# A four-stage graph network on one core: the loop of every engine in each edge pass moved to a multiple of 256 instruction slots

## The reference

```python
x = _layernorm(x + layer(x, edge_index, ...))
# layer 0: two spline convolutions   msg = (1-u)*h0[src] + u*h1[src]; mean over dst
# layer 1: attention; sum, mean and max of messages over dst and again over src
# layer 2: three GCN convolutions, widths 16, 16, 32   sum over dst of norm * h[row]
# layer 3: softmax attention over dst  out = sum(alpha * (z[src] + e)) + x
```

## The kernel before

| from, to | A-B | B-C | C-D | D-E | E-F | F-G | G-H |
|---|---|---|---|---|---|---|---|
| POOL | 185 | 368 | (C-E) 475 | | 165 | 165 | 341 |
| ACT | 103 | 82 | 34 | 129 | 63 | 74 | 118 |
| DVE | 174 | 364 | 259 | 274 | 159 | 181 | 248 |
| PE | 686 | 491 | 281 | 593 | 410 | 548 | 974 |
| SP | 34 | 85 | 40 | 33 | 23 | 23 | 51 |

## Time and profile before

### The profile page before, as it was taken

The page is one execution under the profiler, slowest core; times in us unless marked ns, Lnnn a source line. Parts: engine busy times, 40 slices in busy tenths (PEclk is TensorE's granted clock), DMA queues, the critical chain, the costliest instruction groups (busy, mean ns, idle before and its releaser), DMA issues. The chain is left out here.

```text
span 20591.8 us, 194797 instructions
## 1 busy us (share of the span) xinstructions
PE 7375.4 (36%) x49884; PEld 6283.1 (31%) x49884; DVE 8998.8 (44%) x25746; ACT 2698.1 (13%) x7499; POOL 12080.9 (59%) x11797
## 2 busy tenths in 40 slices
PE   3444444444322232232244544434444444400000
PEld 2333333333232232233211444434443333300000
DVE  3554533333343343344388444444443444333333
ACT  1222212222100000000023111111110111000000
POOL 4666656566566666666611466666665665466664
PEclk9655555555555555555555677767776666555555
DMA  1222212222122222222266000000000000022221
GB/s 56 62 62 62 63 58 80 80 82 84 59 86 81 79 83 84 79 82 81 82 222 234 8 11 12 11 11 11 12 11 19 22 21 21 15 55 56 57 56 42
DMA packets 599140, 1231.22 MB, mean 60 GB/s; under 512 B 229172, under 2 KB 351769, under 8 KB 572838
## 3 DMA queue, kind: packets, MB, share of 16 engines
q0 software_dynamic: 378560, 479.32, 10.7%
q1 hardware_dynamic: 206420, 692.77, 9.3%
q10 hardware_dynamic: 14112, 58.61, 0.8%
HBM read 560.63 MB, written 669.21 MB: 60 GB/s over the span
## 5 line engine op out<-in xcount | busy, mean ns | idle before, releaser
L795 POOL DMA_INDIRECT rows<-gcn_table,index x3430 | 3746.6, 1092 | 2491.0 <-ACT index L803 1509.6
L516 POOL DMA_INDIRECT rows<-spline_table,index x3136 | 3231.6, 1030 | 2038.5 <-ACT index L534 1077.5
L850 PE MATMUL p_slots<-part,lo_t 128*128 128x208 bf16 x18816 | 2549.3, 300 | 2920.8 <-ACT lo_t L812 1809.8
L850 PEld LDWEIGHTS p_slots<-part,lo_t 128*128 128x128 bf16 x18816 | 2007.1, 116 | 3346.1 <-issue 2369.6
L1036 POOL DMA_INDIRECT sent<-a_msg,a_place x1568 | 1578.1, 1006 | 1186.2 <-DVE a_run L1151 712.9
L1378 POOL DMA_INDIRECT e_rows<-soft_table,e_index x1568 | 1520.8, 970 | 845.3 <-issue 491.8
L1028 POOL DMA_INDIRECT a_rows<-att_table,a_index x1568 | 1506.5, 961 | 484.6 <-issue 470.4
L868 DVE TENSOR_TENSOR one_lo<-iota,lo 128x2560 bf16<-128x2560 f32 (+1 forms) x297 | 733.3, 2469 | 2315.5 <-ACT index L803 2125.4
L1092 PE MATMUL a_p_label<-tw,a_label 8*128 8x64 f32 x3136 | 1000.5, 401 | 2036.4 <-issue 1481.1
L1092 PEld LDWEIGHTS a_p_label<-tw,a_label 8*128 8x128 f32 x3136 | 853.2, 318 | 2014.7 <-issue 1728.4
L812 ACT ACTIVATE lo_t<-p_turn 128x512 bf16<-128x512 bf16 x1287 | 719.4, 595 | 5130.8 <-remote 3495.3
(11 more groups left out here) (398 smaller groups left out, 16071.2 us busy)
## 6 DMA issues: line engine op xcount, KB each, us to landing
running_dst<-a_run SPq DMA_DIRECT2D x98, 1600.0 KB
running_src<-s_run SPq DMA_DIRECT2D x98, 1600.0 KB
running<-e_run SPq DMA_DIRECT2D x98, 656.0 KB
s_rows<-sent ACTq DMA_DIRECT2D x98, 584.0 KB
rows<-gcn_table,index POOLq DMA_INDIRECT x3430
running<-run SPq DMA_DIRECT2D x98, 520.0 KB
rows<-spline_table,index POOLq DMA_INDIRECT x3136
running<-run SPq DMA_DIRECT2D x98, 512.0 KB
```

The costliest lines, as they stand in the source:

```text
L516: pool.indirect_dma_start(out=rows[h][:, k, :], out_offset=None, in_=table, in_offset=offsets(index[h][:, k:k + 1])).then_inc(gathered[h], 16)
L795: pool.indirect_dma_start(out=rows[h][:, ON_CHIP + k, :], out_offset=None, in_=table, in_offset=offsets(index[h][:, k:k + 1])).then_inc(ga ...
L850: ins = nc.tensor.matmul(p_slots[:, m, 0:CLASS * SLICE], lo_t[h][:, k, q, :], flat(part[:, c, q * CLASS:(q + 1) * CLASS, :]), start=q == 0 ...
```

## The change

In front of the loop of every engine in all eight passes stands one more call, `addr_align(256)`. It is a directive for the loader: when the program is loaded, no-op instructions are put in until the next slot number is a multiple of 256, and the engine runs through these no-ops, up to 255 of them, each time it comes from the prologue into the loop. That is once per pass and engine. The body of no loop is changed, and what each engine does in it. The slot that is aligned is the register move; the body starts one slot behind it. The loops outside the passes (`dense`) get no directive, but move with the rest. The diff is 24 such lines; its core:

```diff
@@ spline_pass
+            sp.addr_align(256)
             with sp.Fori(0, IT) as i:
...
+            pool.addr_align(256)
             with pool.Fori(0, IT) as i:
...
             stage_index(0, 0)
             stage(0, 0)
+            act.addr_align(256)
             with act.Fori(0, IT) as i:
...
+                pe.addr_align(256)
                 with pe.Fori(0, IT) as i:
...
                 one_hots(0, lambda ins: ins.then_inc(stepped, 1))
+            dve.addr_align(256)
             with dve.Fori(0, IT) as i:
```

## The result

The changed kernel takes 20764.5 us (median of 5 runs, 20744.0 to 20784.1) beside 20665.5 us of the kernel before (5 runs, 20649.2 to 20679.8): ratio 1.0047, 95% interval 1.0033 to 1.0062, 99 us slower. The forecast was +89 us on the median. The two profiled executions lie further apart, 20743.99 and 20593.66 us, because the one of before is shorter than all five of its timed runs.

A forecast was written before the change was run, and what follows sets the result against it. Passes were taken as bound by rings of waits, no engine over 59% busy. Opening no-ops of 92 us less 3 for shorter steps gave +89 on the 20659 us median: 20748 us, range 20655 to 20860.

The forecast's parts named there:

- Part 1: Waits for code inside the loops: code is fetched where a pass opens, never in its turns; term 0.
- faster, by code fetches: Rival: straddling loops fetch code each turn, so aligning saves time: 20590 us, or 20000 at 2 us a turn; chance 0.04.
- Part 2: Step from a loop's end to its head: shorter when aligned, gain at most 39 us, taken as 3 us.
- Part 3: No-ops executed in front of each loop, at 0.064 us each on every engine: 92 us on the path.
- Nothing measurable: Rival: a no-op costs 0.02 us or the loader jumps over the padding, some 25 us in all, 20680 us; chance 0.23.
- twice as dear: Rival: a no-op costs 0.15 us, 234 us in all, 20890 us; chance 0.08.
- A and B, 6.2 and 7.8: Openings of A and B: ACT's no-ops ahead of its first transposes make them 6.2 and 7.8 us later.
- C, 9.5: Opening of C: DVE's 148 no-ops come between turn 0 and the loop while DVE is busy, 9.5 us.
- D, 14.8: Opening of D: PE's 231 no-ops cost 14.8 us, with ACT's 222 and DVE's 253 running at the same time.
- E and F, 15.9 and 15.5: Openings of E and F: PE's no-ops, then ACT's ahead of the index copy, 15.9 and 15.5 us.
- G, 11.5: Opening of G: PE's 220 no-ops less 2.6 us of one-hot, 11.5 us; ACT's 182 covered by its wait.
- H, 10.9: Opening of H: POOL's 171 no-ops ahead of its first gather cost 10.9 us, other engines' beside them.

The follow-up runs named there:

- slot 200: The kernel before with `addr_align(256, offset=200, max_nops=0)` in all 24 places, every loop head at that slot, no no-ops executed: 17344.0 us, ratio 1.0011 to the kernel before.
- doubled: The changed kernel with 256 more no-ops executed by every engine at every pass, same placement: 17534.5 us, ratio 1.0123 to the kernel before.
- chip 11: Batch in which the kernel before, the changed kernel, PE alone and ACT alone were run; the changed kernel took 17415.2 us there, ratio 1.0049 to the kernel before.

## Why the prediction was right, and where it was not

The time (20748 us forecast, 20764.5 measured), the sign and the kind of cause were right: executed no-ops at the openings. Jumped over, the change costs 0.09%; doubled, 1.23%. Point by point:

- **Part 1, no fetches in the turns: right.** Aligned or at slot 200, the instruction queues have about 90 packets for 392 turns, at most two of them inside the turns of all passes. The rival "faster, by code fetches" is out. The rule of the Trainium skill (page "Runtime: NRT & Kernel Launch", section "Instruction fetch mechanics") does not come about as the prediction read it: bodies across a boundary of 256 go round here without a fetch. The rule itself, a stall when a branch's target is no longer held, is not tested. By that section the memory holds 512 instructions on most engines and 2048 on PE (the prediction left PE's out), and the largest bodies here are 234 slots (DVE) and 390 (PE). "A few packets" was too low, 43 more; the jumped kernel, whose padding is not executed, has the same 91, so it is the length of the code and not the execution of the no-ops that brings them.
- **Part 2, a gain of 3 us by the shorter step: wrong in sign.** The steps became as short as read from rows 7, and this cost 30 us in the changed kernel's run on chip 11, through the phase of DVE's `one_lo` against POOL's gathers in F. The prediction named "a moved phase between engines" as what would make it wrong, with 1 us a turn as its size: F had 0.4 to 0.9.
- **Part 3, the price.** 0.064 us for all engines is 0.039 to 0.047 on ACT, POOL and DVE, and 0.072 on PE. The mean hid the difference: terms through ACT are too dear, those through PE too cheap. "Nothing measurable" needed 0.02 and "twice as dear" 0.15, and neither came. By the prediction's own chances "slower by more" comes to 0.62, not 0.65.
- **The counts** were right to the instruction for PE, ACT and DVE from B on, and wrong for POOL: 71, 144, 37, 91, 91, 171 said, 154, 37, 252, 164, 164, 42 found. So POOL's row in the table of distances is wrong: by these counts its distances are 102, 219, 4, 92, 92 and 214 slots above a multiple of 256.
- **A and B, 6.2 and 7.8:** 5 and 0 in the profile after, 6 and 5 on chip 11. The size of A is luck: in the experiments it comes from POOL's no-ops ahead of the first gather and not from ACT's, which alone cost nothing.
- **C, 9.5:** 11 in the profile after, 0 on chip 11. In the experiments POOL's gathers and scatters bound the pass and cover even 20 us of DVE.
- **D, 14.8:** PE's 231 no-ops cost 16.7 us where they run at their pace, with DVE's beside them as forecast. In the profile after they cost 38, where the no-ops of PE and DVE lie in the slow stretch. The 0.7 us steps were in the trace of before, and I had not asked what a no-op costs in one.
- **E and F, 15.9 and 15.5:** 16 and 15 in the profile after, 11 and 7 on chip 11. In the experiments the path is another than forecast: POOL's no-ops alone give 10 and 7, PE's 3 and 1, ACT's 0 and 5.
- **G, 11.5:** 33 in the profile after, with PE's 220 no-ops at 0.13 us each in the mean by steps of 0.7 and 1.4 us; 12 on chip 11, where PE's alone give 5 and POOL's alone 6. ACT's were taken as covered there: alone they cost nothing, so this was right.
- **H, 10.9:** -9 and 2; POOL had 42 no-ops and not 171.
- **"The same time per turn":** wrong. Between the runs of before and after on chip 11 it holds to 3 us in all passes but F. In the profile after E and F took 39.4 us a turn instead of 39.1; PE's products in one ms of E took 318 ns in the mean where they had taken 305 (the median jumps from 253 to 352, because 48% instead of 59% of them take 253 ns), and over E the mean granted clock is 0.69 instead of 0.71 of 2.4 GHz. Whether the change or the execution does this, and what moved A by +52, B by -39 and G by -62 us, stays open: there is one such profile of each kernel. F's rise there is not the one of the experiments: before and after, every gather held at the loop's end starts 0.75 us into `one_lo` and takes 2.89 us.

That the sum came so near is in part luck. On chip 11 the forecast's 92 us of openings stand against 59 us of openings and 30 of F. In the profiles of the result it is 108 us of openings, of which D and G have 71 by the slow steps, and 41 us of turns.

The products of PE in one ms of E, before and after (duration in ns, min/median/max):

```profile
L850 PE MATMUL p_slots<-part,lo_t x3072: 252/253/381, 11999.8 to 12997.5; 128*128 128x208 bf16 x192
```
```profile
L858 PE MATMUL p_slots<-part,lo_t x3047: 252/352/382, 11999.7 to 12996.9; 128*128 128x208 bf16 x191
```

## What to carry to other kernels

Look first whether loops fetch code at all: set the instruction rows of the queue table beside the number of turns. If they don't, there is no fetch for alignment to remove. Padding that is executed costs its count times the engine's own price on every engine whose first work the opening waits for, and the engine that feeds the gathers is one of them. If a place is wanted, let the engine jump over the padding. And where two engines hold each other up, a step that changes by 0.02 to 0.1 us on one of them can shift a ring of waits into a form that is up to 0.9 us longer in each turn: compare the time of each pass, not the total alone.

## What the runs showed of the hardware that I had not expected

- A row gather of POOL that starts 0.05 to 1.3 us after DVE's `one_lo` (128x2560, 2.83 us) ends only 0.8 us behind it: 3.59 us when it starts 0.05 us after, 3.49 at 0.15, 2.42 at 1.3, against 0.94 otherwise. At 0.03 or 0.04 us after, 212 of 525 are not held; ahead of it none is.
- A no-op costs 72 ns on PE and 37 to 47 on the others, nearly the same in every run outside the slow stretches.
- A part of code is 16 KB on the queue that carries PE's (q8) and 8 KB on the other (q14): 0.26 MB in 16 and in 32 packets. PE's no-ops alone bring 4 more packets on q8 and none on q14.
- In the two profiles of the result the instructions of PE, DVE and SP, no-ops among them, are at times 0.7 or 1.4 us apart while POOL sends gathers back to back; in the experiments this is almost absent, and the same kernel takes 17325 instead of 20665 us. Whether that is the chip or something else is open. The ratio of the two kernels is the same in both places, 1.0047 and 1.0049.
